# The local branch's values computed by tokens, in two halves around the last part of the down projection

## The reference

```python
out_c = softmax(compressed-block logits) @ v_c          # 32 blocks of 16 tokens
out_s = softmax(logits over the 4 best blocks) @ v_s    # selected branch
wmask = (abs(pos[:, None] - pos[None, :]) <= WIN // 2) & (pos[:, None] >= pos[None, :])
out_l = softmax(where(wmask, q @ k.T / scale, NEG)) @ v # local branch, WIN // 2 = 32
gates = softmax(q.mean(axis=1) @ Wg + bg)
out = gates[0] * out_c + gates[1] * out_s + gates[2] * out_l      # then @ Wo
mlp = silu(h @ Wg + bg) * (h @ Wu + bu) @ Wd + bd       # 1024 wide
experts = sum over 4 heads of the 8 best of 1024 experts: silu(h . down) * weight * up
```

## Time and profile before

| | |
|---|---|
| time, median of 3 runs | 1492.09 us (1492.06 to 1493.76) |
| the profiled execution | 1490.08 us, of which span 1488.3 us |
| mean granted TensorE clock | 0.981 of full speed |
| PE, share of the span | 94% |
| DVE | 77% |
| ACT, POOL | 62%, 64% |
| DMA, mean over the span | 76 GB/s |

### The profile page before, as it was taken

How to read it: one execution, slowest core, us unless ns; L and a number is a source line. 1 busy time by engine, 2 the same in 40 slices (tenths; PEclk the granted TensorE clock), 3 DMA queues, 4 the chain that set the end, 5 groups by cost and what they waited for, 6 DMA issues and landing times. The chain is left out here.

```text
span 1488.3 us, 43616 instructions
## 1 busy us (share of the span) xinstructions
PE 1399.5 (94%) x14864; PEld 1041.1 (70%) x14960; DVE 1148.8 (77%) x4512; ACT 927.1 (62%) x1684; POOL 946.8 (64%) x877
## 2 busy tenths in 40 slices
PE   6899569999999999999999999999999999999978
PEld 4566437777777777777777777777777777777757
DVE  5444378888888888888888888888888888888712
ACT  3776436666666666666666666666666666666641
POOL 4655357777777766666666666666676666666720
PEclk8999969999999999999999999999999999999989
DMA  6556842211112222222212222122222222222027
GB/s 187 202 192 213 269 82 54 52 44 48 46 47 51 52 52 52 52 50 47 47 47 47 50 52 47 48 52 52 52 52 52 52 52 52 66 52 53 9 83 250
DMA packets 217149, 113.76 MB, mean 76 GB/s; under 512 B 128872, under 2 KB 211224, under 8 KB 217112
## 3 DMA queue, kind: packets, MB, share of 16 engines
q1 hardware_dynamic: 216304, 112.88, 27.9%
q10 hardware_dynamic: 808, 0.42, 0.2%
HBM read 73.08 MB, written 40.16 MB: 76 GB/s over the span
## 5 line engine op out<-in xcount | busy, mean ns | idle before, releaser
L1394 DVE TENSOR_REDUCE bmax<-q_bank 128x32 f32<-128x512 f32 (+3 forms) x512 | 221.2, 487 | 34.4 <-PE q_bank L1635 34.2
L1149 POOL TENSOR_TENSOR sumxy<-xy 128x1024 f32<-128x1024 f32 x128 | 246.1, 1942 | 0.0
L1241 ACT ACTIVATE pts<-k_bank 128x512 f32<-128x512 f32 (+2 forms) x384 | 177.4, 490 | 42.2 <-PE k_bank L1670 41.4
L1115 POOL TENSOR_TENSOR pad<-pad 128x1 f32<-128x1 f32 x32 | 6.2, 193 | 287.4 <-DVE top L1413 287.4
L1495 DVE SCALAR_TENSOR_TENSOR mw<-sumxy,c,ex 128x1024 f32<-128x1024 f32 x128 | 162.0, 1287 | 13.4 <-ACT ex L1259 9.6
L1617 PE MATMUL f_bank<-xt,wfu 128*128 128x128 f32 x1024 | 162.4, 281 | 0.0
L1635 PE MATMUL q_bank<-ko,qo 96*128 96x512 bf16 (+3 forms) x512 | 142.6, 306 | 16.9 <-DVE bmax L1394 16.7
L1175 POOL TENSOR_TENSOR cw<-cw,mw 128x1024 f32<-128x1024 f32 x64 | 150.9, 2358 | 11.5 <-ACT mw L1265 8.9
L1617 PE MATMUL f_bank<-xt,wfg 128*128 128x128 f32 x1024 | 150.3, 279 | 0.0
L1617 PEld LDWEIGHTS f_bank<-xt,wfu 128*128 128x128 f32 x1024 | 139.4, 191 | 11.5
L1318 ACT ACTIVATE oT<-k_bank 128x512 f32<-128x512 f32 x64 | 38.2, 597 | 173.8 <-PE k_bank L1685 129.3
(11 more groups left out here) (211 smaller groups left out, 3307.8 us busy)
## 6 DMA issues: line engine op xcount, KB each, us to landing
qo<-s_qs SPq DMA_DIRECT2D x192, 64.0 KB, 2.2
ko<-s_ks SPq DMA_DIRECT2D x186, 64.0 KB, 2.2
s_qs<-parts SPq DMA_DIRECT2D x8, 768.0 KB, 4.7
s_ks<-parts SPq DMA_DIRECT2D x8, 768.0 KB, 6.3
s_v<-vo SPq DMA_DIRECT2D x8, 544.0 KB, 3.0
vv<-s_v SPq DMA_DIRECT2D x32, 136.0 KB, 2.3
vw<-s_v SPq DMA_DIRECT2D x64, 68.0 KB, 2.5
xin<-in_L_attn_x_dram SPq DMA_DIRECT2D x8, 512.0 KB, 7.1
```

The costliest lines, as they stand in the source:

```text
L1149: done("sum_done", g_.tensor_tensor(sumxy[:, h, :, :], xy[:, 0, h, 0:XK, None].broadcast_to([P, XK, KEYS]), xy[:, 1, h, None, :].broadcast ...
L1241: last = s.activation(pts[:, h, OFFS[j]:OFFS[j] + n], bank[:, 0:n], ACT.Exp)
L1394: last = v.tensor_reduce(bmax[:, i, h, 0:n], Q.bank(job)[:, o:o + n * BLK].rearrange("p (n j) -> p n j", j=BLK), AX.X, ALU.max)
```

## The change

The local values are computed by tokens: `pT` (64 positions by 32 tokens) is now the stationary operand and `vw` (64 by 17) the moving one, so the result has tokens on partitions and 17 columns for each head and tile of tokens in bank `vl`. DVE's `normalize(t, 1)` reads `vl` directly, with a spacing of 17 columns. Bank job `tl`, `token_values(t, 1)` and ACT's copy of the local values are gone; ring K has 23 jobs.

Where the old call did all 64 matmuls in one go at the end of head 2, the new one is called twice: row group r = 0 (heads 0 and 1, partitions 0 to 63), then r = 1, 32 matmuls each. The two write the same partitions of one bank. Between them stands `mlp_down(t, 3)`, moved from part 3 of head 3; its last matmul waits by the new semaphore `vl_half` until the first half is complete. All of this stands behind the windows and ahead of the selected values. `local_ready` moves to head 3, part 2. On DVE `normalize(t, 1)` moves behind `local_scores` and `selected_max`. POOL's `branches` waits for `vl` in place of `tl`.

```diff
-                k_jobs += [f"s{h}0", f"s{h}1", f"s{h}2"] + [f"a{h + 1}"] * (h < HG - 1) + [("pl0", "pl1", "vl", "tl")[h]]
-            k_jobs += ["vs", "ts"]
+                k_jobs += [f"s{h}0", f"s{h}1", f"s{h}2"] + [f"a{h + 1}"] * (h < HG - 1) + [f"pl{h}"] * (h < 2)
+            k_jobs += ["vl", "vs", "ts"]
...
-                    K.wait_read(pool, t, "tl")
+                    K.wait_read(pool, t, "vl")
...
-                    elif h == 2:
-                        branch_values(t, 1)
...
-                    job = ("ts", "tl")[k]
+                    job, w = (("ts", 32), ("vl", VW))[k]
...
-                    normalize(t, 1)
                     if n:
                         local_scores(n, now=t)
                         selected_max(n)
+                    normalize(t, 1)
+                    if n:
                         pair_sums(n)
...
-                def local_values(t):
+                def local_values(t, r):
 
                     bank = K.bank("vl")
-                    for g in range(T // 32):
-                        for h in range(HG):
-                            rows, k = slice(64 * (h // 2), 64 * (h // 2) + 64), h % 2
-                            last = mm(bank[32 * h:32 * h + VW, 32 * g:32 * g + 32], vw[rows, t.half, g, VW * k:VW * k + VW],
-                                      pT[rows, k, 32 * g:32 * g + 32], start=True, stop=True, skip_group_check=True)
-                    K.filled("vl", last)
+                    rows = slice(64 * r, 64 * r + 64)
+                    for k in range(2):
+                        for g in range(T // 32):
+                            i, q = divmod(g, 4)
+                            o = VW * (HG * i + 2 * r + k)
+                            last = mm(bank[32 * q:32 * q + 32, o:o + VW], pT[rows, k, 32 * g:32 * g + 32],
+                                      vw[rows, t.half, g, VW * k:VW * k + VW], start=True, stop=True, skip_group_check=True)
+                    if r == 0:
+                        done("vl_half", last)
+                    else:
+                        K.filled("vl", last)
...
                     for f in (2 * part, 2 * part + 1):
+                        if f == FT - 1:
+                            need(pe, "vl_half", t)
                         mm(Y.bank("y")[:, 0:C], hT[:, f, :], wfd[:, f, :], start=(f == 0), stop=False)
...
-                            elif h == 2:
-                                local_ready(t)
-                            else:
-                                token_values(t, 1)
                             if h < 3:
                                 up_rows(t, "ugu"[h], (0, 1, 1)[h], part)
-                            else:
+                            elif part < 3:
                                 mlp_down(t, part)
-                            if (h, part) == (2, 3):
-                                local_values(t)
+                            if (h, part) == (3, 2):
+                                local_ready(t)
...
                         window(n, 1)
+                    local_values(t, 0)
+                    mlp_down(t, 3)
+                    local_values(t, 1)
                     selected_values(t)
                     transposed_weights(t)
                     experts_down(t, 0)
-                    token_values(t, 0)
+                    token_values(t)
                     experts_down(t, 1)
```

More of the change, by code:

```diff
@@ L914, in build @@
             vw = sb("vw", [P, 2, T // 32, 2 * VW])
-            oT = sb("oT", [P, 2, T])
+            oT = sb("oT", [P, T])
             fs = sb("fs", [P, TT, HG])
@@ L966, in build @@
                     ("pc_exp", 1, 0), ("cfac_done", 1, 0), ("pc_done", 1, 0),
-                    ("smax_done", 1, 0), ("shift_lo", 1, 0), ("wl_exp", 1, 0), ("shift_top", 1, 0),
+                    ("smax_done", 1, 0), ("shift_lo", 1, 0), ("wl_exp", 1, 0), ("vl_half", 1, 0), ("shift_top", 1, 0),
                     ("xb_done", 1, 0), ("bsel_done", 1, 0), ("at_sum", 1, 0), ("at_done", 1, 1),
@@ L1313, in openings, with selected_values @@
                     tanh(t, "g0", hidden(0), "th_done")
[L1315 to L1318, removed]
+                def selected_values(t):
+                    K.wait_full(act, t, "vs")
+                    K.released("vs", s.activation(oT[:, :], K.bank("vs")[:, :], ACT.Copy))
                 def lead(n):
@@ L1351, in step @@
                         e8_exp(n)
-                    branch_values(t, 0)
+                    selected_values(t)
                     for j in range(2):
@@ L1509, in normalize @@
                 def normalize(t, k):
-                    job = ("ts", "tl")[k]
+                    job, w = (("ts", 32), ("vl", VW))[k]
                     K.wait_full(dve, t, job)
-                    bank = K.bank(job)[:, :].rearrange("p (i h w) -> p i h w", i=TT, h=HG)
-                    cf.link(v.reciprocal(bank[:, :, :, D], bank[:, :, :, D]))
-                    cf.link(v.tensor_tensor(fs[:, :, :], bank[:, :, :, D],
+                    bank = K.bank(job)[:, 0:TT * HG * w].rearrange("p (n w) -> p n w", w=w)
+                    cf.link(v.reciprocal(bank[:, :, D], bank[:, :, D]))
+                    cf.link(v.tensor_tensor(fs[:, :, :], bank[:, :, D].rearrange("p (i h) -> p i h", i=TT),
                                             gt[:, t.half, :, 1 + k:2 + k].broadcast_to([P, TT, HG]), ALU.mult))
@@ L1519, in normalize @@
                     K.released(job, v.tensor_tensor(on[:, k, :, :, :].rearrange("p i h d -> p (i h) d"),
-                                           K.bank(job)[:, :].rearrange("p (n w) -> p n w", w=32)[:, :, 0:D],
+                                           bank[:, :, 0:D],
                                            fs[:, :, :].rearrange("p i h -> p (i h)")[:, :, None].broadcast_to([P, TT * HG, D]),
@@ L1713, in local_shares, with token_values @@
                     K.filled(f"pl{k}", last)
[L1715 to L1719, removed]
+                def token_values(t):
+                    K.wait_read(pe, t, "vs")
+                    K.wait_free(pe, t, "ts")
                     for i in range(TT):
-                        last = tr(K.bank(job)[:, P * i:P * i + P], oT[:, k, P * i:P * i + P], ident[:, :])
-                    K.filled(job, last)
+                        last = tr(K.bank("ts")[:, P * i:P * i + P], oT[:, P * i:P * i + P], ident[:, :])
+                    K.filled("ts", last)
                 def compressed(t):
```

## The result

| | before | changed |
|---|---|---|
| time, median of 4 runs | 1492.62 us (1492.06 to 1493.76) | 1502.66 us (1499.71 to 1504.72) |
| the profiled execution | 1490.08 us, span 1488.3 | 1499.71 us, span 1498.0 |
| ratio | | 1.0064, 95% interval 1.005 to 1.0078 |

The changed kernel is 0.64% slower, 10.0 us by the medians and 9.6 by the profiled executions. In the code of after the lines are shifted by 2 to 4: `result` is L1525, `up` L1382, `block_max` L1391, `local_values` L1703 as before, `mlp_down` L1770, `window` L1644 and L1655, the selected values L1683.

The account below looks back on a forecast made before the run. PE is busy 94%, but DVE's reductions were taken to set the first window's start: 26.95 + 9.21 + 2.40 = 38.56 us a step against 38.40, about +5 us; 1492.09 + 5 + 0.5 = 1497.6 us, range 1488 to 1509.

Parts of the forecast that it names:

- m0 is set by DVE, at 26.95 us: First window job on PE starts only after DVE's reduction of p30, 26.95 us after L1528.
- PE alone would have given 38.06: Step if only PE's own work counted: 38.40 - 2.74 + 2.40 = 38.06 us, that is -0.34.
- The tail grows by 2.40 us: PE's work from the first window to the next L1528, 9.21 us before, gets 2.40 us longer.
- a: From the window to the first half: change of array tiles, 0.12 us in place of 0.02.
- b: Each half of the local values, 64 instructions on PE: 0.50 us, twice 1.00.
- c: Out of the first half into `mlp_down`: 0.13 plus 0.08 for an fp32 load that can't run ahead, 0.21 us.
- d: `mlp_down` part 3 behind the windows: 0.86 us, its wait on `vl_half` hidden.
- e: From `mlp_down` part 3 into the second half: 0.10 us, as before the old block.
- f: Out of the second half to the selected values at L1685: 0.13 us.
- A: Rival, chance 0.22: the halves' price is at its low end, nothing measurable left; 1492, or 1489.5 with quite cheap halves.
- B: Rival, chance 0.12: PE stays the bound, DVE arriving earlier or halves running faster; 1481, with fast halves 1484.
- C: Rival, chance 0.04 including half-way forms: the halves' loads on one row group don't overlap; step 2.3 us longer, 1569.

Follow-up runs that it names:

- e1: Changed kernel with DVE's `unselected` moved from ahead of `up` to behind head 3's three reductions; 1493.74 us, ratio 1.000.
- e3: Changed kernel plus one more DVE reduction over 512 columns, result unused, right ahead of `up(t, 1)`; 1523.86 us, ratio 1.0189.
- e2: Kernel before with DVE's `unselected` moved from ahead of `up` to behind head 3's three reductions; 1491.75 us, ratio 0.9988.
- e4: Kernel before plus one more DVE reduction over 512 columns, result unused, right ahead of `up(t, 1)`; 1493.33 us, ratio 0.9997.
- e9: Changed kernel with only `mlp_down` part 0 moved ahead of head 3's first scores; 1500.41 us, ratio 1.0065.
- e5: Kernel before with only `mlp_down(t, 3)` moved behind the two windows; 1501.11 us, ratio 1.0069.
- e7: Changed kernel with both halves moved ahead of the windows and `mlp_down` part 3 back at its old place; 1489.53 us, ratio 0.9987.
- e8: Changed kernel with halves ahead of the windows, `mlp_down` part 3 back, and part 0 ahead of head 3's first scores; 1481.34 us, ratio 0.9927.
- e6: The changed kernel itself, run again beside other kernels; 1506.6 us, ratio 1.0104.
- e10: The changed kernel itself, run once more for its scatter; 1504.06 us, ratio 1.0074.

## Why the prediction was right, and what was missed

The forecast was 1497.6 us, slower with 0.63, between 1488 and 1509; measured 1502.66. The way is as forecast: DVE sets m0, and the gain was eaten where it was said. The size is short by 4.5 us (5.5 forecast, 10.0 measured). One step of the working was wrong, what PE would reach alone; that it did little harm to the sum, because DVE set m0 all the same, is luck.

*m0 is set by DVE, at 26.95 us.* Right: 26.91. e1 and e3 show it from both sides, e2 and e4 that the kernel before had the time in hand. The idle time ahead of it lies elsewhere than I said, though. I had 0.20 us before `mlp_down` part 2 and 0.34 before m0; there are 0.21 ahead of head 3's first scores (below), 0.07 inside part 2's burst (1.10 for 1.03) and 0.19 before m0. The sign "idle, released by L1385, before `mlp_down`" shows in e3 and e9 and not in the changed kernel.

*PE alone would have given 38.06.* Wrong: with DVE out of the way (e1) the step is 38.41, no better than before. Of the 0.35 that are missing 0.21 are the wait for a3 below and 0.10 the longer tail.

*The tail grows by 2.40 us.* Nearly: from m0 to the selected values it is 748.55 - 744.83 = 3.72 us now and 743.46 - 742.24 = 1.22 in the earlier trace rows, so 2.50. By its terms, forecast and measured: a 0.12 and 0.11; b 0.50 and 0.54 for each half (0.73 - 0.19); c 0.21 and 0.13 + 0.10; d 0.86; e 0.10 and 0.10 (746.83 to 747.89 is 1.06, c's load and e included); f 0.13 and 0.12. Only b was clearly sized too low: 8.6 ns an instruction, between the two rows it was taken from. The wait on `vl_half` is hidden, as said: the burst of part 3 is 1.13, as in e5, where it waits for no half.

*Rivals.* A and B fell with the tail and with e1. C, loads that don't overlap on one row group, asked for more than 12 ns an instruction, and priced a load that doesn't overlap at 26: it is 8.6 with all four tiles of a half on the same 64 rows. The Trainium skill ("TensorE: Matmul & The Clock Gate", Part 3, The mechanism) says that a load overlaps only when the row group differs; the trace goes against it for tiles of different columns. The Trainium skill ("TensorEngine Tiling (Array Packing)", Key Properties) says that a change of tiling mode drains the engine; the trace agrees at each of the four places of the new tail, with 0.10 to 0.13 us.

*What was missed.* First, an edit costed at nothing: the old block had covered ACT's copy of a3. Head 3's first scores wait for it, now that nothing stands between: the up rows end at 739.88 + 0.71 - 0.28 + 0.11 = 740.42, L1668 starts at 740.63. The waits of the loads name it: `L1668 <- ACT qo L1307`, 4.2 us in the changed kernel and in e7, where the kernel before and e8 have one single wait there:

```profile
...
PEld k_bank L1670 <- ACT qo L1309: 0.3, 1, 0.3
...
```

In the changed kernel these 0.21 us only take the place of waits for DVE, as e9 shows. Where PE is the bound, covering them is worth 8 us by the medians, as e7 and e8 show; by the mean steps it is 0.33, of which 0.21 are the wait and 0.08 the load of `mlp_down` part 0, covered there too (its burst is 1.11 in e7 and 1.03 in e8). I had named what waits for the removed copy on ACT, but not what the removed block of PE had been hiding. With the longer tail it is also why the last step did not get its -0.34 (33.11, 33.12 before).

Second, three single events of PE in the middle of a half, with nothing in the profile that it waited for. The first, of 0.92 us at 243.85, stands ahead of the first `result`; the others are in the next step and in the last one with windows:

```profile
...
284.74 0.37 PE L1703 MATMUL k_bank<-vw,pT 64*32 64x17 f32 x22 [0.42 <-issue]
...
1402.65 0.60 PE L1703 MATMUL k_bank<-vw,pT 64*32 64x17 f32 x49
1404.43 0.31 PE L1703 MATMUL k_bank<-vw,pT 64*32 64x17 f32 x15 [1.19 <-issue]
...
```

In the kernel before the last such step has 0.53 us of this kind, at an `mlp_down`. They were in no view of before that I had read for the sum. The other two profiles of the changed kernel (e6, e10) have the first two events as well, 0.6 to 1.4 us between starts, and nothing at the third place: their last step with windows takes 38.3 us, where the first profile has 39.7. So the first two belong to the first two steps of this kernel, and the third is of one execution. e7 has none, e8 one. Their cause stays open.

The sum of the profiled executions: steady steps are 38.60 and 38.66 in turn, 38.63 (38.36 to 38.46 before, 38.39 on average; 28 steps: 6.6 us); the first interval between two `result`s and the last one with windows carry 0.9 and 1.0 more; from the first to the last `result` that is 1193.5 us against 1185.1, so 8.4 (7.3 and 7.1 in e6 and e10). The first `result` comes 1.3 later. 9.7 in all, the difference of the spans. Against the 5 forecast this is 4.7 more: 2.1 in the 28 steps, which are 0.24 longer and not 0.16 (the tail 0.11 more, m0 0.04 earlier, the base 38.39 for 38.40, since the mean of 17 steps held one long step); 1.5 for the two steps with events in the loop; 1.2 ahead of the first `result`; 0.3 for the last step; less 0.4, by which I had rounded 4.6 up to 5.

## What to carry to other kernels

Work that is moved from in front of a point of meeting to behind it counts in full for the chain of the other engine; what decides is the time which that engine has in hand at the point, read from its waits, not the busy share. The waits of the weight loads show a short stall of PE that its matmuls hide. Before taking a block out of an engine's order, list what waits for other engines right behind it: the block may be the cover. Put small tiles and full-width matmuls in few runs: each change of kind cost 0.10 us here, and a 128-column fp32 load that can't run ahead another 0.10.

## What the runs showed of the hardware

`shift_top`'s tensor operation on DVE (L1455, two SBUF inputs of 128x16) takes 0.70 us in the step of the kernel before and 1.88 in the changed one, with the same operands; its shortest is 0.23. In the changed kernel it runs beside Pool's second sum and ends with it (Pool 747.71 + 3.75 = 751.46, DVE 749.67 + 1.88 = 751.55):

```profile
...
749.67 1.88 DVE L1455 TENSOR_TENSOR shift_s<-smax,smax_hi 128x16 bf16<-128x16 f32 x1
...
```

```profile
...
747.71 3.75 POOL L1149 TENSOR_TENSOR sumxy<-xy 128x1024 f32<-128x1024 f32 x2
...
```

In the kernel before it runs beside a shorter operation of Pool and again ends 0.09 after it (747.39 and 747.30):

```profile
...
746.69 0.70 DVE L1458 TENSOR_TENSOR shift_s<-smax,smax_hi 128x16 bf16<-128x16 f32 x1
...
```

```profile
...
746.58 0.72 POOL L1185 TENSOR_TENSOR xb<-xb,bdb 128x256 f32<-128x256 f32 x1
...
```

The Trainium skill ("SBUF — State Buffer", Terms) says that DVE and GpSimd arbitrate for one pair of ports, that the lock is exclusive and held for a whole instruction, and that the loser blocks; by that rule DVE waits for the end of Pool's running operation, and the trace agrees. This one costs nothing in the changed kernel's tail, since DVE waits 2 us for the turned selected values after it.

`unselected` matters more, since it stands in the chain that sets m0. It takes 1.97 us as written, about 1.2 in e1 and 0.42 in e2, with the same operands. Its first instance in the kernel before, ahead of the loop, takes 0.43. In the changed kernel it starts 0.22 after the first of two sums of Pool (739.97) and ends at 742.16, 0.29 after that sum, which ends near 741.87, where the second starts:

```profile
...
740.19 1.97 DVE L1442 TENSOR_SCALAR unsel<-struck 128x512 bf16<-128x512 f32 x1
...
```

```profile
...
741.83 2.09 POOL L1149 TENSOR_TENSOR sumxy<-xy 128x1024 f32<-128x1024 f32 x1
...
```

```profile
...
742.61 0.42 DVE L1447 TENSOR_SCALAR unsel<-struck 128x512 bf16<-128x512 f32 x1
...
```

The last line is e2's, where none of Pool's long operations runs beside it. So up to 1.5 us of the chain to m0 may be a wait for Pool, several times the 0.22 us that this chain costs in a step. No run was made to separate Pool's part in it.
